# Scores on two halves of TensorE's rows, and the attention steps of a chunk dealt out to two half steps

## The chip, the cores and the metric

The kernel runs on one core of one Trainium2 chip. The time is the device time of one launch, in microseconds (us). Engines work side by side, each through its own list of instructions in order, and meet only at semaphores: TensorE (PE, with its weight loads PEld), VectorE (DVE), ScalarE (ACT), GpSimd (POOL) and SyncE (SP), which here only issues DMAs.

## The reference

The input x has 64 sequences of 128 tokens and 256 features; ctx has 192 features per token. One layer of cross attention with two softmaxes, then a quantised feed-forward layer:

```
x = x + attention(layernorm(x), ctx)      # 16 heads of 64
    q = x @ Wq + lora;  k, v = ctx[:124] @ Wk, Wv + lora
    out  = softmax(q k^T / 8) v           # the first 124 context tokens
    out += softmax(q ki^T / 8) vi         # the last 4, with Wk_ipa, Wv_ipa
    result = out @ Wo + bo + lora
x = x + ffn(layernorm(x))
    h = silu(depthwise_conv3(bitlinear(x, w1)));  bitlinear(h, w2)
```

`bitlinear` rounds its input to 8 bits by row and its weights to -1, 0, 1.

## The kernel before

**Tiling.** Four sequences make a group (`NB = 4`), so there are 16 groups. Within a group, attention goes by chunks: one sequence b and one quad q of four heads, 16 chunks to a group (`CHUNKS`). Each chunk has two half steps, so a group has 32 halves, numbered n = 0 to 31.

**Order.** Every engine has a function `steps(g, n)`, called for each group and each half, and the order of calls in it is the engine's order. Attention of group g, the projections of group g + 1 (`project`) and the feed-forward part of group g - 1 (`finish`) are interleaved by tables of half numbers (`N_Q`, `N_K`, `M_TILE`, ...). Groups 0 and 1 and the last stand unrolled; the others run in a hardware loop.

**A chunk s before**, all of it in even halves:
- PE, n = 2s: `p_v` of chunk s - 3 (L438), `transpose_p` of chunk s - 2 (L447), `scores` of chunk s (L460), `project_out` of chunk s - 4 (L473). After them and in the odd half come the projections (Q L403, K L412, V L422) and the feed-forward matmuls (L485 to L517).
- DVE, n = 2s: `attend`: the sum of the four extra exponentials and the reciprocals of chunk s - 1 (L800, L802), then the maxima of chunk s and the subtraction (L805, L806, L808). Then `project` and `finish`.
- ACT, n = 2s: the two copies of the output of chunk s - 3 (L636, L638), the copy of the transposed P of chunk s - 2 (L630), then `project` and `finish`, and at the end of the half the exponentials of chunk s (L644 four times, L647).
- POOL, n = 2s: P times the reciprocals for chunk s - 1 (L1029); in the odd half the low part of the output of chunk s - 3 (L1061).

**DVE's other work by half**, from the tables: statistics in 0 and 1; rounding of the hidden layer (L887, L894) in 1 to 3; variance in 3; `x2` (L827) in 4 and 7; normalisation in 6 to 10; V copies (L793) in 5, 14, 22 and 29; nothing in 11, 12, 13 and 31; convolution (L851, L857, L866, L871) in 15 to 27, one of these in 15 and in 27; maxima of the hidden layer (L876) in 28 and 29; scales (L880 and on) in 30. The second feed-forward matmul (L517) is in PE's halves 4 and 6; the result of 4 is used by L818 in 6, and the second run of L517 in 6 waits for that L818.

**Heads.** The keys KT of a pair of heads fill the 128 partitions, 64 for each head. A score matmul before contracts over all 128: the query tile QM holds each pair twice, with zeros in the half of the other head. ACT fills it with two copies (L611, L612), and POOL sets the zeros once at the start (L1048, L1050). P times V already writes its heads to two halves of the PSUM partitions, that is of the array's columns.

**PSUM.** Before, bank 0 holds the scores, bank 1 the transposed P, bank 2 the output of P times V, banks 3 and 4 the output product, 5 and 6 the projections, 7 the feed-forward part.

## Time and profile before

| | us |
|---|---|
| median of 3 runs (1666.96 to 1673.72) | 1671.57 |
| the profiled execution | 1673.32 |
| its span | 1671.2 |
| PE busy | 1474.9 (88%) |
| DVE busy | 1305.2 (78%) |
| ACT busy | 1183.1 (71%) |
| POOL busy | 729.1 (44%) |

The profile is of one execution. Busy time is the share of the span in which an engine has an instruction in flight; for PE the ends are modelled and neighbours overlap. "[4.32 <-PE PS L460]" behind an instruction says that its engine had been idle for 4.32 us, and that the matmul of line 460 ended the wait. DMAs move 28 GB/s on average and are of no weight in the loop.

### The profile page before, as it was taken

The page shows a single profiled execution, that of the slowest core. Times are in us where ns is not written, and L with a number is a line of the kernel's source. Part 1 is how long each engine was busy: PE and PEld are TensorE (multiplying, and loading weights), DVE is VectorE, ACT ScalarE, POOL GpSimd, SP SyncE. Part 2 cuts the span into 40 slices and gives each one's busy share as a digit, 9 for nine tenths or more (in the row PEclk, how much of TensorE's full clock was granted, in tenths as well). Part 3 has the DMA queues.
Part 4 walks back from the last instruction along what each step waited for, and adds up shares of the span by engine and source line. Part 5 has one row for each costly group of instructions (what it writes and reads, how often), then busy time and mean ns, then how long its engine had stood idle before and what let it go on. Part 6 is the DMA issues. An engine that isn't in the chain of part 4 may idle for free.

```text
span 1671.2 us, 33198 instructions
## 1 busy us (share of the span) xinstructions
PE 1474.9 (88%) x10586; PEld 1168.1 (70%) x10586; DVE 1305.2 (78%) x3157; ACT 1183.1 (71%) x3925; POOL 729.1 (44%) x1085
## 2 busy tenths in 40 slices
PE   7999999989899998989899998989999898988642
PEld 3688777777777777777777777777777777776521
DVE  4264798888878798787879888887878878787876
ACT  2477776868677786968778686867778696876521
POOL 0144445444544444444444544454444445444400
PEclk9899999999999999999999999999999999999855
DMA  7300001000000100000010100000010000000000
GB/s 187 117 28 15 28 15 42 15 25 15 26 27 13 40 13 27 13 26 27 13 40 13 40 10 27 17 26 27 13 40 13 27 13 26 27 1 26 1 13 13
DMA packets 41129, 47.14 MB, mean 28 GB/s; under 512 B 3008, under 2 KB 35200, under 8 KB 41088
## 3 DMA queue, kind: packets, MB, share of 16 engines
q1 hardware_dynamic: 40032, 45.82, 8.9%
q10 hardware_dynamic: 1056, 0.81, 0.2%
q8 instruction: 22, 0.36, 0.1%
q14 instruction: 19, 0.16, 0.0%
HBM read 36.13 MB, written 10.49 MB: 28 GB/s over the span
## 4 chain that ended last, share of the span: by engine, by line
PE 35%; DVE 32%; ACT 20%; issue 11%; DMA 0%; POOL 0%; DVEq 0%; ACTq 0%; POOLq 0%
ACT SM L644 8%; DVE GBS L876 7%; PE PS L460 6%; PE PS L422 4%; PE PS L517 4%; PE PS L403 4%; PE PS L438 4%; PE PS L447 3%; PE PS L412 3%; PE PS L473 3%; DVE GBS L887 2%; ACT H L669 2%; DVE GBS L866 2%; ACT GBS L674 2%; DVE H L894 2%
## 5 line engine op out<-in xcount | busy, mean ns | idle before, releaser
L1029 POOL TENSOR_TENSOR SM<-SM,RC 128x496 f32<-128x496 f32 (+1 forms) x512 | 340.3, 686 | 730.5 <-DVE RC L802 730.5
L644 ACT ACTIVATE SM<-PS,MX 128x124 f32<-128x124 f32 x1024 | 359.3, 365 | 200.1 <-DVE SM L808 197.1
L460 PE MATMUL PS<-KT,QM 128*128 128x128 f32 x2048 | 279.2, 279 | 26.3 <-ACT SM L644 26.2
L460 PEld LDWEIGHTS PS<-KT,QM 128*128 128x128 f32 x2048 | 249.4, 192 | 42.7 <-ACT SM L644 41.5
L1061 POOL TENSOR_TENSOR OTl<-OF,OTh 128x256 fp32r<-128x256 f32 x256 | 216.4, 846 | 5.6 <-ACT OF L638 5.6
L644 ACT ACTIVATION_READ_ACCUMULATOR SM<-PS,MX 128x1 f32 x1024 | 211.0, 206 | 0.0
L447 PE MATMUL PS<-IDF,SM 128*128 128x128 f32 x1024 | 169.3, 288 | 18.9 <-POOL SM L1029 18.8
L636 ACT ACTIVATE OTh<-PS 128x256 fp32r<-128x256 f32 x256 | 99.6, 389 | 103.2 <-PE PS L438 99.4
L438 PE MATMUL PS<-PT,V 128*64 128x128 f32 x2048 | 170.2, 288 | 0.0
L806 DVE TENSOR_REDUCE MX<-PS 128x4 f32<-128x496 f32 x256 | 169.9, 664 | 0.0
L438 PEld LDWEIGHTS PS<-PT,V 128*64 128x64 f32 x2048 | 107.8, 137 | 83.5 <-issue 77.0
L630 ACT ACTIVATE PT<-PS 128x512 f32<-128x512 f32 x256 | 155.6, 608 | 0.8 <-PE PS L447 0.7
L447 PEld LDWEIGHTS PS<-IDF,SM 128*128 128x128 f32 x1024 | 108.3, 142 | 65.5 <-issue 35.9
L473 PE MATMUL PS<-WOh,OTh 128*128 128x256 f32 x512 | 124.7, 325 | 17.1 <-POOL OTl L1061 17.1
L866 DVE TENSOR_TENSOR GBS<-PS,BC 128x512 f32<-128x512 f32 x128 | 87.5, 683 | 60.9 <-PE PS L498 58.3
L805 DVE TENSOR_REDUCE MX<-PS 128x4 f32<-128x16 f32 x256 | 41.3, 161 | 110.4 <-PE PS L460 110.4
L669 ACT ACTIVATE H<-GBS,CB,CW 128x512 f32<-128x512 f32 x128 | 105.3, 823 | 29.0 <-DVE GBS L866 27.7
L871 DVE SCALAR_TENSOR_TENSOR H<-GBS,H 128x512 f32<-128x512 f32 x128 | 103.4, 808 | 27.1 <-ACT GBS L674 27.0
L638 ACT ACTIVATE OF<-PS 128x256 f32<-128x256 f32 x256 | 99.5, 389 | 31.2 <-POOL OTl L1061 31.2
L876 DVE TENSOR_REDUCE GBS<-H 128x128 f32<-128x1024 f32 x64 | 120.5, 1928 | 0.0
L851 DVE SCALAR_TENSOR_TENSOR H<-GBS,CW,H 128x508 f32<-128x508 f32 x128 | 116.4, 909 | 0.0
L857 DVE SCALAR_TENSOR_TENSOR H<-GBS,CW,H 128x508 f32<-128x508 f32 x128 | 107.9, 843 | 10.4 <-ACT H L669 8.8
(142 smaller groups left out, 3693.8 us busy)
## 6 DMA issues: line engine op xcount, KB each, us to landing
XIN<-in_x SPq DMA_DIRECT2D x16, 512.0 KB, 3.6
XRES<-in_x SPq DMA_DIRECT2D x16, 512.0 KB, 3.5
out_y<-H SPq DMA_DIRECT2D x16, 512.0 KB, 3.0
CRAW<-in_ctxT SPq DMA_DIRECT2D x16, 256.0 KB, 2.8
RRAW<-in_ctxT SPq DMA_DIRECT2D x32, 128.0 KB, 2.8
QM<-in_Wq SPq DMA_DIRECT2D x1, 1024.0 KB, 11.0
GBS<-in_Wo SPq DMA_DIRECT2D x1, 1024.0 KB, 21.6
k_ipa_columns<-H SPq DMA_DIRECT2D x1, 1024.0 KB, 5.1
```

What stands on the lines that cost most here:

```text
L438: m = mm(psO[r:r + DH, h // 2, :], V[:, b, DH * (4 * q + h):DH * (4 * q + h) + DH], PT[:, h, :], start=True, stop=True)
L447: m = pe.transpose(psT[:, h, :], SM[c % 2][:, h, :], IDF[:])
L460: m = mm(psS[:, h, :], QM[:, 2 * q + h // 2, h % 2, TOK * b:TOK * b + TOK], KT[:, 2 * q + h // 2, b, :], start=True, stop=True)
L473: m = mm(psY[b // 2][:, b % 2, :], OT[ot][c % 2][:, a, :], WO[w][:, 2 * q + a, :], start=(q == 0 and i == 0 and b % 2 == 0), stop=(q == QU ...
L630: act.activation(PT[:], psT, ACT.Identity).then_inc(pt_done, 1)
L644: m = act.activation(SM[s % 2][:, h, 0:ORG], psS[:, h, 0:ORG], ACT.Exp, bias=MX[s % 2][:, h:h + 1], accum_out=SU[s % 2][:, h:h + 1])
L669: act.activation(H[:, j, :].rearrange("p (b t) -> p b t", b=NB), GB[j % 4], ACT.Identity, bias=CB[:, j:j + 1], scale=CW[:, j, 1:2]).then_i ...
L806: dve.tensor_reduce(MX[s % 2][:, 0:4], psS[:, :, 0:ORG], AX.X, ALU.max, negate=True)
L866: dve.tensor_tensor(GB[j % 4].rearrange("p b t -> p (b t)"), psF, BC[:], ALU.mult).then_inc(g_done, 1)
L876: dve.tensor_reduce(HM[:, b, :], H[:, :, TOK * b:TOK * b + TOK].rearrange("p j t -> p t j"), AX.X, ALU.max, apply_absolute_value=True).the ...
L1029: m = pool.tensor_tensor(part, part, RC[c % 2][:, 4 * i:4 * i + 4].unsqueeze(2).broadcast_to(shape), ALU.mult)
L1061: pool.tensor_tensor(OT[1][c % 2][:], OF[:], OT[0][c % 2][:].bitcast(F32), ALU.subtract).then_inc(ot_done, 1)
```

## The change

- **Scores.** QM becomes QT, with each pair of heads once. A head's scores contract over its own 64 partitions, on its own half of the array's rows; even heads write PSUM bank 0, odd heads bank 1. ACT needs one copy of a query tile in place of two (128 partitions in place of twice 64), and the zeros go. A tile STAGE takes over the weight staging that QM did at the start.
- **Banks.** The scores hold banks 0 and 1, so the transposed P moves to bank 2, the bank that the output of P times V lies in. So `transpose_p` now waits for the output copies of the chunk before (`ot_high`), and `p_v` no longer does.
- **Halves.** `transpose_p` and `scores` (PE), the copy of the transposed P and the exponentials (ACT) and the maxima and the subtraction (DVE, now the function `maxima`) move to the odd half n = 2s + 1. `p_v`, `project_out`, the output copies, the sums and reciprocals (DVE, now `sums`) and POOL's steps stay in the even one.

```diff
-        psS = PS[:, 0, :].rearrange("p (h k) -> p h k", h=4)
-        psT = PS[:, 1, :].rearrange("p (h k) -> p h k", h=4)
+        psS = PS[:, 0:2, 0:2 * TOK].rearrange("p r (a k) -> p r a k", a=2)
+        psT = PS[:, 2, :].rearrange("p (h k) -> p h k", h=4)
...
# PE, p_v
-                    need(pe, ot_high, gc.count(CHUNKS, c))
...
# PE, transpose_p
                     pe.wait_ge(p_done, gc.count(CHUNKS, c + 1))
+                    need(pe, ot_high, gc.count(CHUNKS, c))
...
# PE, scores
-                        m = mm(psS[:, h, :], QM[:, 2 * q + h // 2, h % 2, TOK * b:TOK * b + TOK],
-                               KT[:, 2 * q + h // 2, b, :], start=True, stop=True)
+                        rows = slice(DH * (h % 2), DH * (h % 2) + DH)
+                        m = mm(psS[:, h % 2, h // 2, :], QT[rows, 2 * q + h // 2, TOK * b:TOK * b + TOK],
+                               KT[rows, 2 * q + h // 2, b, :], start=True, stop=True)
...
# PE, steps
                 if n % 2 == 0:
                     p_v(g, n // 2)
+                    project_out(g, n // 2)
+                else:
                     transpose_p(g, n // 2)
                     scores(g, n // 2)
-                    project_out(g, n // 2)
...
# ACT, project
-                        act.activation(QM[0:64, 2 * q + a, 0, :], psU[u % 2][0:64, :], ACT.Identity)
-                        act.activation(QM[64:128, 2 * q + a, 1, :], psU[u % 2][64:128, :], ACT.Identity).then_inc(unit_free[u % 2], 1)
+                        act.activation(QT[:, 2 * q + a, :], psU[u % 2], ACT.Identity).then_inc(unit_free[u % 2], 1)
...
# ACT, steps
                 if n % 2 == 0:
                     output_copies(g, n // 2)
+                else:
                     transposed_copy(g, n // 2)
...
-                if n % 2 == 0:
+                if n % 2 == 1:
                     exponentials(g, n // 2)
...
# DVE, steps
                 if n % 2 == 0:
-                    attend(g, n // 2)
+                    sums(g, n // 2)
+                else:
+                    maxima(g, n // 2)
...
# POOL, at the start
-            pool.memset(QM[0:64, :, 1, :], 0.0).then_inc(zeroed, 1)
-            pool.wait_ge(zeroed, 1)
-            pool.memset(QM[64:128, :, 0, :], 0.0).then_inc(zeroed, 1)
```

The DVE's list in halves 4 and 5 of a group, before: SU and RC are the sums and reciprocals, MX and the SM row the maxima and the subtraction.

```order
L800 TENSOR_REDUCE SU<-SM 128x4 [waits exp_done]
L802 RECIPROCAL RC<-SU 128x8 [waits sum_done]
L804 REGISTER_ALU
L805 TENSOR_REDUCE MX<-PS 128x4 [waits s_full]
L806 TENSOR_REDUCE MX<-PS 128x4
L808 TENSOR_TENSOR SM<-PS,MX 128x4x4 [waits max_done]
L823 REGISTER_ALU
L824 ISA [waits y_done]
L120 REGISTER_ALU [waits xres_done]
L827 TENSOR_TENSOR X<-PS,XRES 128x512 [waits copy_done]
L792 ISA
L793 COPY V<-PS 124x2x256 [waits unit_full]
```

The same place on the DVE in the changed kernel (lines are some 1 to 3 higher there).

```order
L801 TENSOR_REDUCE SU<-SM 128x4 [waits exp_done]
L803 RECIPROCAL RC<-SU 128x8 [waits sum_done]
L826 REGISTER_ALU
L827 ISA [waits y_done]
L120 REGISTER_ALU [waits xres_done]
L830 TENSOR_TENSOR X<-PS,XRES 128x512 [waits copy_done]
L807 REGISTER_ALU
L808 TENSOR_REDUCE MX<-PS 128x4 [waits s_full]
L809 TENSOR_REDUCE MX<-PS 128x4
L811 TENSOR_TENSOR SM<-PS,MX 128x4x4 [waits max_done]
L793 ISA
L794 COPY V<-PS 124x2x256 [waits unit_full]
```

The maxima moved from right behind the sums to behind the even half's other work, so that only the odd half's work (here the copy of V) stands between them and the next sums.

ACT's list from half 12 to 14, before: OTh and OF are the two output copies, PT the transposed P, the SM rows the exponentials, Q1T a copy of the feed-forward part.

```order
L636 ACTIVATE OTh<-PS 128x256 [waits o_full]
L638 ACTIVATE OF<-PS 128x256 [waits ot_done]
L630 ACTIVATE PT<-PS 128x512 [waits t_full]
L616 REGISTER_ALU
L617 ACTIVATE KT<-PS 128x4x124 [waits unit_full]
L642 REGISTER_ALU
L644 ACTIVATE SM,SU<-PS,MX 128x124 [waits sub_done]
L644 ACTIVATE SM,SU<-PS,MX 128x124 x3
L647 ACTIVATE SM<-SM 128x4x4
L636 ACTIVATE OTh<-PS 128x256 [waits o_full]
L638 ACTIVATE OF<-PS 128x256 [waits ot_done]
L630 ACTIVATE PT<-PS 128x512 [waits t_full]
```

ACT in the changed kernel, from half 12 to 14.

```order
L636 ACTIVATE OTh<-PS 128x256 [waits o_full]
L638 ACTIVATE OF<-PS 128x256 [waits ot_done]
L616 REGISTER_ALU
L617 ACTIVATE KT<-PS 128x4x124 [waits unit_full]
L630 ACTIVATE PT<-PS 128x512 [waits t_full]
L642 REGISTER_ALU
L644 ACTIVATE SM,SU<-PS,MX 128x124 [waits sub_done]
L644 ACTIVATE SM,SU<-PS,MX 128x124 x3
L647 ACTIVATE SM<-SM 128x4x4
L636 ACTIVATE OTh<-PS 128x256 [waits o_full]
L638 ACTIVATE OF<-PS 128x256 [waits ot_done]
```

The copy of PT and the exponentials now stand at the two ends of an odd half, and the output copies follow the exponentials directly.

PE's list from the second feed-forward product in half 4 on, before.

```order
L517 MATMUL PS<-W,H 128x256 [waits q2_done]
L517 MATMUL PS<-W,H 128x256 x15
L403 MATMUL PS<-XTh,WQh 128x512 [waits unit_free1]
```

PE at the same place in the changed kernel.

```order
L518 MATMUL PS<-W,H 128x256 [waits q2_done]
L518 MATMUL PS<-W,H 128x256 x15
L447 MATMUL PS<-IDF,SM 128x128 [waits ot_high,p_done]
L447 MATMUL PS<-IDF,SM 128x128 x3
L120 REGISTER_ALU
L461 MATMUL PS<-KT,QT 128x128 [waits s_used]
L461 MATMUL PS<-KT,QT 128x128 x3
L403 MATMUL PS<-XTh,WQh 128x512 [waits unit_free1]
```

The transposes and scores moved from ahead of that product (they stood at the start of half 4, and stand next at the start of half 6) to right behind it.

## Rows read from the trace of the kernel before

**Rows 1.** Busy us by engine in one stretch, instructions; clock, DMA share, GB/s.

```profile
800.00:900.00 100.00, 92.25 (x691) 74.25 (x690) 83.74 (x206) 77.23 (x260) 47.76 (x71) 1.00 0.07 22
```

**Rows 2.** Timeline, DVE: start, us, line, operation; L805 of group 2, then of 15.

```profile
248.89 0.17 DVE L805 TENSOR_REDUCE MX<-PS 128x4 f32<-128x16 f32 x1 [1.43 <-PE PS L460]
...
1492.15 0.17 DVE L805 TENSOR_REDUCE MX<-PS 128x4 f32<-128x16 f32 x1
```

**Rows 3.** Waits between 700 and 1000 us: who for whom, total us, times, longest.

```profile
ACT SM L644 <- DVE SM L808: 36.9, 21, 4.6
...
DVE MX L805 <- PE PS L460: 15.3, 19, 1.9
...
DVE SU L800 <- ACT SM L647: 6.4, 6, 1.7
```

**Rows 4.** Timeline, DVE, first two chunks of group 0.

```profile
85.88 0.17 DVE L805 TENSOR_REDUCE MX<-PS 128x4 f32<-128x16 f32 x1 [4.32 <-PE PS L460]
...
88.39 0.17 DVE L800 TENSOR_REDUCE SU<-SM 128x4 f32<-128x16 f32 x1 [0.35 <-ACT SM L647]
...
89.50 0.17 DVE L805 TENSOR_REDUCE MX<-PS 128x4 f32<-128x16 f32 x1 [0.70 <-PE PS L460]
```

**Rows 5.** Timeline, ACT, first chunk of group 0.

```profile
86.75 0.37 ACT L644 ACTIVATE SM<-PS,MX 128x124 f32<-128x124 f32 x1 [0.77 <-DVE SM L808]
...
88.13 0.23 ACT L647 ACTIVATE SM<-SM 128x16 f32<-128x16 f32 x1
```

**Rows 6.** Timeline, ACT, a chunk of the loop.

```profile
863.87 0.23 ACT L647 ACTIVATE SM<-SM 128x16 f32<-128x16 f32 x1
863.98 0.39 ACT L636 ACTIVATE OTh<-PS 128x256 fp32r<-128x256 f32 x1
864.24 0.40 ACT L638 ACTIVATE OF<-PS 128x256 f32<-128x256 f32 x1
```

**Rows 7.** Timeline, PE, a chunk of the loop.

```profile
839.76 0.40 PE L403 MATMUL PS<-XTl,WQh 128*128 128x512 f32 x1
839.99 0.40 PE L403 MATMUL PS<-XTh,WQl 128*128 128x512 f32 x1
840.32 0.66 PE L438 MATMUL PS<-PT,V 128*64 128x128 f32 x8
840.91 0.66 PE L447 MATMUL PS<-IDF,SM 128*128 128x128 f32 x4
841.40 1.06 PE L460 MATMUL PS<-KT,QM 128*128 128x128 f32 x8
842.21 0.48 PE L473 MATMUL PS<-WOh,OTh 128*128 128x256 f32 x2
```

**Rows 8.** Timeline, DVE, the same chunk.

```profile
842.50 0.17 DVE L805 TENSOR_REDUCE MX<-PS 128x4 f32<-128x16 f32 x1 [1.86 <-PE PS L460]
```

**Rows 9.** Timeline, PE, the second feed-forward product.

```profile
837.07 1.92 PE L517 MATMUL PS<-W,H 128*128 128x256 bf16 x16 [0.45 <-DVE H L894]
838.75 0.47 PE L403 MATMUL PS<-XTh,WQh 128*128 128x512 f32 x1
```

**Rows 10.** Timeline, PE, half 13.

```profile
860.76 0.28 PE L422 MATMUL PS<-WVh,CTh 128*128 128x256 f32 x1
...
861.93 0.62 PE L485 MATMUL PS<-IDB,H 128*128 128x128 bf16 x8
```

**Rows 11.** Timeline, DVE, half 28.

```profile
811.34 3.85 DVE L876 TENSOR_REDUCE GBS<-H 128x128 f32<-128x1024 f32 x2
```

**Rows 12.** Timeline, DVE and POOL, the convolution.

```profile
880.02 1.23 DVE L871 SCALAR_TENSOR_TENSOR H<-GBS,H 128x512 f32<-128x512 f32 x1
...
882.90 0.68 DVE L871 SCALAR_TENSOR_TENSOR H<-GBS,H 128x512 f32<-128x512 f32 x1
...
879.48 1.22 POOL L1061 TENSOR_TENSOR OTl<-OF,OTh 128x256 fp32r<-128x256 f32 x1
```

**Rows 13.** Lines of ACT: count, busy us, mean ns, idle before.

```profile
L612 ACT ACTIVATE QM<-PS 64x512 f32<-64x512 f32 x128 | 75.9, 593 | 1.5
```

More of the change, by code:

```diff
@@ L170, in program @@
         CTR = sb("CTR", [P, T], F32R)
-        QM = sb("QM", [P, PAIRS, 2, T])
+        QT = sb("QT", [P, PAIRS, T])
+        STAGE = sb("STAGE", [P, 4096])
         KT = sb("KT", [P, PAIRS, NB, TOK])
@@ L224, in program @@
         kv_full, kv_used, ipa_out = sem("kv_full"), sem("kv_used"), sem("ipa_out")
-        zeroed = sem("zeroed")
         x_in, c_in = sem("x_in"), sem("c_in")
@@ L260, in program @@
         kipa_dram = nc.dram_tensor("k_ipa_columns", [GROUPS, P, PAIRS * NB * IPA], F32, kind="Internal").ap()
-        qm_flat = QM[:].rearrange("p a b t -> p (a b t)")
-        wq_raw = qm_flat[:, 0:2048].rearrange("p (k n) -> p k n", k=2)
-        wk_raw, wkr_raw, wv_raw, wvr_raw = (qm_flat[:, 2048 + 1024 * i:3072 + 1024 * i] for i in range(4))
-        q_up_t, k_up_t = (qm_flat[:, 6144 + 1024 * i:7168 + 1024 * i] for i in range(2))
+        wq_raw = STAGE[:, 0:2048].rearrange("p (k n) -> p k n", k=2)
+        q_up_t, k_up_t = (STAGE[:, 2048 + 1024 * i:3072 + 1024 * i] for i in range(2))
+        qt_flat = QT[:].rearrange("p a t -> p (a t)")
+        wk_raw, wkr_raw, wv_raw, wvr_raw = (qt_flat[:, 1024 * i:1024 * i + 1024] for i in range(4))
         kt_flat = KT[:].rearrange("p a b t -> p (a b t)")
@@ L438, in p_v @@
                         m = mm(psO[r:r + DH, h // 2, :], V[:, b, DH * (4 * q + h):DH * (4 * q + h) + DH],
-                               PT[:, h, :], start=True, stop=True)
+                               PT[:, 2 * (h % 2) + h // 2, :], start=True, stop=True)
                     m.then_inc(o_full, 1)
@@ L563, in _ @@
                 project(At(0), n)
-            pe.wait_ge(zeroed, 2)
             pe.wait_ge(w_low, len(splits))
@@ L643, in exponentials @@
                     for h in range(4):
-                        m = act.activation(SM[s % 2][:, h, 0:ORG], psS[:, h, 0:ORG], ACT.Exp, bias=MX[s % 2][:, h:h + 1],
+                        m = act.activation(SM[s % 2][:, h, 0:ORG], psS[:, h // 2, h % 2, 0:ORG], ACT.Exp, bias=MX[s % 2][:, h:h + 1],
                                            accum_out=SU[s % 2][:, h:h + 1])
@@ L794, in project, with sums @@
                                     psU[u % 2][0:ORG, :].rearrange("p (b n) -> p b n", b=2)).then_inc(unit_free[u % 2], 1)
-            def attend(g, s):
+            def sums(g, s):
                 gc, c = chunk_at(g, s - 1)
@@ L802, in attend, with maxima @@
                     dve.reciprocal(RC[c % 2][:], SU[c % 2][:]).then_inc(rec_done, 1)
+            def maxima(g, s):
                 if g.exists():
                     dve.wait_ge(s_full, g.count(CHUNKS, s + 1))
-                    dve.tensor_reduce(MX[s % 2][:, 4:8], psS[:, :, ORG:TOK], AX.X, ALU.max, negate=True).then_inc(max_done, 1)
-                    dve.tensor_reduce(MX[s % 2][:, 0:4], psS[:, :, 0:ORG], AX.X, ALU.max, negate=True)
+                    dve.tensor_reduce(MX[s % 2][:, 4:8].rearrange("p (r a) -> p r a", r=2), psS[:, :, :, ORG:TOK], AX.X, ALU.max, negate=True).then_inc(max_done, 1)
+                    dve.tensor_reduce(MX[s % 2][:, 0:4].rearrange("p (r a) -> p r a", r=2), psS[:, :, :, 0:ORG], AX.X, ALU.max, negate=True)
                     dve.wait_ge(max_done, g.count(CHUNKS, s + 1))
-                    dve.tensor_tensor(SM[s % 2][:, :, ORG:TOK], psS[:, :, ORG:TOK],
-                                      MX[s % 2][:, 4:8].unsqueeze(2).broadcast_to([P, 4, IPA]), ALU.add).then_inc(sub_done, 1)
+                    dve.tensor_tensor(SM[s % 2][:, :, ORG:TOK].rearrange("p (r a) k -> p r a k", r=2), psS[:, :, :, ORG:TOK],
+                                      MX[s % 2][:, 4:8].rearrange("p (r a) -> p r a", r=2).unsqueeze(3).broadcast_to([P, 2, 2, IPA]), ALU.add).then_inc(sub_done, 1)
             def finish(g, n):
@@ L1044, in _ @@
                 project(At(0), n)
-            pool.wait_ge(w_low, 6)
-            pool.wait_ge(du_used, DU_O)
-            pool.memset(QM[0:64, :, 1, :], 0.0).then_inc(zeroed, 1)
-            pool.wait_ge(zeroed, 1)
-            pool.memset(QM[64:128, :, 0, :], 0.0).then_inc(zeroed, 1)
-            pool.wait_ge(zeroed, 2)
             pool.wait_ge(du_used, DU_N)
```

## The prediction

> **What bounds the kernel now.** First the busy time of the engines in a stretch of the loop [rows 1]: TensorE (PE) 92.3 us of 100, VectorE (DVE) 83.7, ScalarE (ACT) 77.2, at the full granted clock (1.00). None is full. PE's busy time counts overlapping matmuls double, so the DVE, whose operations run one behind the other, is the better ruler. The time of one group of 16 chunks comes from the first and last start of the small maximum (L805) over groups 2 to 14, which run all stages together [rows 2]: (1492.15 - 248.89) / 13 = 95.6 us, 5.98 us per chunk. Of these the DVE works 95.6 x 0.84 = 80.3 us and idles 15.3 us. The waits of 300 us [rows 3] show that it idles little for anything: 15.3 us for the scores in 19 waits, 6.4 us for the exponentials in 6, while ACT waits for the DVE's subtraction 36.9 us in 21. So the DVE leads; ACT and PE follow, and each has slack to it because the DVE's sums read exponentials which ACT made a whole half (two halves are one chunk) earlier.
>
> I therefore write the time of a group as DVE work plus DVE idle; the work stays, and the idle time is built anew for the changed order.
>
> **The serial chain.** In group 0 nothing else delays the chunks, and their pieces can be read off [rows 4, 5]. From L805 (85.88) to the first exponential (86.75) is 0.87 us; the last one's end lets the DVE start its sums at 88.39, so L805 to L800 takes 2.5 us. The next L805 comes at 89.50: 3.6 us per chunk is the shortest cycle before.
>
> After the change two things lengthen it. First, the exponentials of a chunk are the last thing in ACT's odd half, and the sums are the first thing in the DVE's next even half: in the odd half the DVE can hide only 2.5 - 0.73 (its maxima, L805 to the next operation) = 1.77 us by its own work. Second, the transposes now share bank 2 with P times V, and wait for `ot_high`. ACT makes the two output copies right after the exponentials. In the loop [rows 6], after L647 starts (863.87), L636 and L638 follow at 0.11 and 0.37 us, L638 lasts 0.40, so the copies are done 0.77 us after L647's start. Sums begin 0.26 us after L647's start [rows 4, 5], so the copies end 0.5 us behind the sums' start. Then transposes to scores 0.49 us (840.91 to 841.40), scores to L805 1.10 us (841.40 to 842.50) [rows 7, 8]. Scores on two halves of the rows change only the last number. Behind the waiting transposes stand the scores, and the DVE's maxima wait for these.
>
> **Price of the scores.** Eight matmul passes of four heads take 0.81 us (841.40 to 842.21), 0.10 us each. No row shows two row halves. The nearest is P times V, on two halves of the columns: eight passes in 0.59 us (840.32 to 840.91), 0.07 us each, though with half as many weight columns. If the halves overlap fully, 0.40 us go: scores to L805 0.7 us. If they don't overlap and PE has to switch its layout in and out, it costs what entering P times V costs more than a plain step, (840.32 - 839.99) - (839.99 - 839.76) = 0.10 us, and as much again: 1.3 us. I take 1.0 us, nearer to the P times V row. So from the sums' start to the next L805 are 0.5 + 0.05 + 0.49 + 1.0 = 2.0 us (1.7 to 2.3); less the sums (0.3), the DVE can hide 1.7 us by its even half. The shortest chunk becomes 2.5 + 2.0 = 4.5 us.
>
> The Trainium skill, TensorEngine Tiling, Key Properties, says that a change of tiling mode drains TensorE; the rows of P times V agree with a small cost, 0.10 us. By full overlap, as its Theoretical Speedup has it (up to twice), the chunk would be 4.2 us, by drains alone 4.8.
>
> **Idle of the DVE per group, half by half** (n is the half; the work in each follows from the placement numbers). The terms are what of 1.8 us (exponentials, odd half) and of 1.7 us (next scores, even half) the work there leaves open.
>
> - 31 and 0: no work in 31, 0.7 us in 0 (two statistics): 1.8 + 1.0 = 2.8.
> - 3 and 4: the second output product (L517) waits for the DVE's rounding, takes 1.7 us (837.07 to 838.75) [rows 9], and now stands ahead of the transposes of half 5: 1.7 + 0.5 + 1.0 + 0.1 = 3.3 us behind the rounding, in which the DVE has 1.4 us of work: 1.9.
> - 5 and 6: 0.6 us of work in 5 leaves 1.2; in 6 the next L517 waits for L818 behind the sums, and the transposes again for it: 0.8 + 3.3 us against 2.1 of work: 2.0. Together 3.2.
> - 11 and 12: no work at all: 1.8 + 1.7 = 3.5.
> - 13 and 14: PE sets the pace. Projection of V 1.17 (860.76 to 861.93), transposes 0.6 (L485) [rows 10], then Q 1.4 (six steps of 0.23), the broadcast 0.9 (an estimate: two passes of a float32 matmul four times as long as a score pass), P times V and product 1.4, less 0.3 because they start ahead of L805 (842.21 against 842.50), transposes and scores 1.5: 6.7 us against 1.0 + 0.6 of the DVE: 5.0.
> - 15 and 16: in the same way 5.9 us of PE against 3.7: 2.2.
> - 25 and 26: 1.4 us of work in each, 0.4 + 0.3 = 0.7. 27: one operation of 0.6, 1.2. 30: L880 needs PE's transposes of the maxima, which the DVE's own maxima of scores hid before: 0.5.
> - 1, 2, 7 to 10, 17 to 24, 28, 29: the work is longer than what is to be hidden (two L876 alone are over 3.7 us [rows 11]): 0.
>
> Sum 21.0 us. Added to it is 1.2 us of slower DVE work: L871 took 0.68 us alone and 1.23 us beside L1061 on GpSimd [rows 12]. The multiplication L1029 ran beside the maxima, which read PSUM; now it runs beside the even half's work from SBUF. Bounds 0 and 0.5 x 16 = 8 us; I take 0.3 us in each of the four conv chunks.
>
> A group: 80.3 + 21.0 + 1.2 = 102.5 us, 6.9 more than 95.6 (22.2 us of idle and slowed time in place of 15.3). Times 13: 90. Groups 1 and 15 have most stages: 5 each. Group 0 is bound by PE and this chain, 3 us. Sum 103 us.
>
> **What costs nothing.** ACT saves one copy of 0.59 us per tile (L612, 128 of them, 75.9 us) [rows 13]; ACT waits for the DVE anyway, so it only waits more. The memsets of the query tile (GpSimd, 3.5 us each) lie beside the first projections. DMAs are unchanged in size and time.
>
> The profiled execution took 1673.3 us, 2.1 us beyond its span, and 1.7 over the median shown. 1673.3 + 103 = 1776 us.
>
> **The rivals.**
> - Faster: the scores leave the path. The DVE's waits for L460 [rows 3] are 15.3 us in 3 groups, 5.1 per group, and if ACT and DVE hide the handshake by the slack of the next half, those go: 16 x 5 = 80 us at most, of which I would keep 40: 1635. For it: PE is the busiest. Against: the exponentials and sums adjoin, and no slack is left there. It decides if the DVE finds the exponentials finished in halves 12 and 0. 0.11.
> - No change: the PE saving pays for the handshake, 1665 to 1681. 0.05.
> - Halves don't run together: 0.3 us more in the seven chunks where the scores are on the path, and 0.1 in others: 3 us a group, about 1825. For it: the switch rows; against: the cheaper passes of P times V. 0.17.
> - GpSimd contention in every chunk: 5 us a group more, 1850. The slowed L871 speaks for it, the many DVE operations that read PSUM against. 0.05.
> - Mild: full overlap (0.3 less in seven chunks) and PE running ahead in 3 to 6: 3 us a group less, 1725. 0.22.
>
> The forecast itself, 1750 to 1800, has 0.40. Range: 1670 to 1830, which leaves out the faster case, the contended one and little else. This kernel's measurement tells about 0.5% (8 us) from no change. Faster 0.11, same 0.05, slower 0.84.
>
> **What would show it.** L801 (sums) waiting for ACT's exponentials in over half of the chunks, some 1.2 to 1.8 us each in halves 0, 6, 12, 28; the transposes waiting for ACT's L638; the shortest chunk 4.5 us; eight score passes in 0.4 to 0.8 us; DVE busy down to 78 of 100. I am wrong if sums still rarely wait, or if the group takes under 97 us.

## The result, and the profile after

The changed kernel takes 1844.6 us (median of 4 runs, 1842.4 to 1846.4) against 1671.4 us for the kernel before (4 runs): a ratio of 1.104, 95% interval [1.102, 1.106]. The direction was forecast, the size not: 173 us in place of 103, beyond the upper end of 1830. The profiled execution's span is 1842.6 us, and the mean granted clock 0.929 (before 0.967).

The view of busy time by engine over the same 100 us as in [rows 1], of the changed kernel (columns as there):

```profile
800.00:900.00 100.00, 85.07 (x614) 64.31 (x610) 76.83 (x180) 63.20 (x218) 44.48 (x65) 0.95 0.07 22
```

Every engine is less busy: PE 92 to 85, DVE 84 to 77, ACT 77 to 63. No engine became the bound; all of them wait more. Of the last three figures (granted clock, DMA share, GB/s) the first has fallen too: 0.95 where it was 1.00.

The period of a group, from the small maximum (now L808) of groups 2 and 15, as in [rows 2]:

```profile
261.91 0.17 DVE L808 TENSOR_REDUCE MX<-PS 128x4 f32<-128x16 f32 x1 [1.17 <-PE PS L461]
...
1654.18 0.17 DVE L808 TENSOR_REDUCE MX<-PS 128x4 f32<-128x16 f32 x1 [1.82 <-PE PS L461]
```

The first row starts at 261.91 and the other at 1654.18: (1654.18 - 261.91) / 13 = 107.1 us, forecast 102.5, before 95.6. Who waits for whom between 700 and 1000 us, as in [rows 3]:

```profile
ACT SM L644 <- DVE SM L811: 50.4, 39, 4.9
...
DVE MX L808 <- PE PS L461: 32.2, 14, 5.1
...
DVE SU L801 <- ACT SM L647: 20.8, 17, 1.7
PE PS L447 <- ACT OF L638: 19.8, 13, 4.8
DVE H L860 <- ACT H L669: 10.8, 12, 1.4
```

ACT waits for the DVE's subtraction in nearly every chunk, and the DVE for ACT's exponentials in 17 of some 45: 20.8 us where [rows 3] had 6.4. The prediction had asked for over half of the chunks. Over the whole run it is 106 chunks of 256, 127.5 us, 1.2 us each: the length came out as forecast, the number of chunks did not. The third row from the top of this list is the handshake that was forecast, the next the shared bank. The last is one that was not.

The DVE's intervals from one L808 to the next, named by their odd half (31 is the one with half 0 in it), forecast and then the mean over groups 2 to 14, in us:

| 31 | 1 | 3 | 5 | 7 | 9 | 11 | 13 |
|---|---|---|---|---|---|---|---|
| 4.5 | 8.7 | 5.9 | 7.1 | 6.2 | 8.7 | 4.5 | 6.7 |
| 4.72 | 9.07 | 5.80 | 7.09 | 6.18 | 9.58 | 5.42 | 7.96 |

| 15 | 17 | 19 | 21 | 23 | 25 | 27 | 29 |
|---|---|---|---|---|---|---|---|
| 5.9 | 5.8 | 6.2 | 6.8 | 5.5 | 4.6 | 6.6 | 8.4 |
| 6.01 | 5.64 | 6.70 | 6.42 | 6.62 | 4.85 | 6.52 | 8.50 |

The prediction doesn't list these intervals. The forecast line was worked out after the result, from the prediction's idle terms and the DVE's work in each interval; this work adds up to 81.1 us, where the prediction has 80.3. Nine of the sixteen lie within 0.25 us of it. Four are over 0.8 us off: 9, 11, 13 and 23. They make 4.2 of the 5.0 us between the sums of the two lines (102.1 and 107.1; the prediction's own sum, with its contention, was 102.5).

Halves 12 to 14 on PE, from its timeline (start, us, line, tiles; in brackets the idle time before), in one group (interval 13 takes 8.54 us here, more than its mean):

```profile
835.26 0.39 PE L474 MATMUL PS<-WOh,OTl 128*128 128x256 f32 x2
838.97 1.09 PE L447 MATMUL PS<-IDF,SM 128*128 128x128 f32 x4 [3.31 <-ACT OF L638]
839.98 1.23 PE L461 MATMUL PS<-KT,QT 64*128 64x128 f32 x8
841.14 0.58 PE L422 MATMUL PS<-WVh,CTh 128*128 128x256 f32 x1
...
843.44 1.08 PE L486 MATMUL PS<-IDB,H 128*128 128x128 bf16 x8
...
848.51 0.60 PE L447 MATMUL PS<-IDF,SM 128*128 128x128 f32 x4
849.04 0.71 PE L461 MATMUL PS<-KT,QT 64*128 64x128 f32 x8
849.69 0.50 PE L412 MATMUL PS<-CTh,WKh 128*128 128x512 f32 x1
```

and the busy times by stretch there (PE, PEld, DVE, ACT, POOL, then the granted clock):

```profile
836.00:838.00 2.00, 0.00 (x0) 0.00 (x0) 0.64 (x2) 1.32 (x8) 0.00 (x0) 1.00 0.83 218
838.00:840.00 2.00, 1.03 (x6) 0.73 (x6) 0.37 (x2) 1.30 (x6) 1.20 (x3) 0.63 0.13 44
840.00:842.00 2.00, 2.00 (x13) 1.78 (x13) 0.74 (x3) 0.60 (x1) 1.09 (x4) 0.50 0.00 0
842.00:844.00 2.00, 2.00 (x14) 1.91 (x14) 0.30 (x4) 1.60 (x9) 0.00 (x0) 0.50 0.00 0
844.00:846.00 2.00, 2.00 (x17) 1.53 (x16) 0.75 (x2) 0.43 (x2) 1.19 (x2) 0.67 0.00 0
846.00:848.00 2.00, 2.00 (x11) 1.58 (x10) 0.00 (x0) 1.14 (x2) 1.43 (x2) 1.00 0.00 0
```

PE idles 3.31 us, since the transposes wait for ACT's copy of O. In this group the granted clock is 0.50, the 1.2 GHz level, for about 6.8 us: all of 840 to 844 and, by the clocks 0.63 and 0.67, some 1.5 and 1.3 us of the windows on both sides, so that it fell before the idle time was over. The same transposes and scores, T and S below, take 1.01 and 1.16 us there (838.97 to 839.98 to 841.14), and 0.53 and 0.65 at full clock (848.51 to 849.04 to 849.69). The stretch lies in the intervals 11 (835.81 to 841.26) and 13 (to 849.80), in which little of the DVE's work hides it.

Interval by interval, in groups 2 to 14, three things show that this is more than one bad group. The clock is under 1 in intervals 11 and 13 of every group (0.50 to 0.81 and 0.75 to 0.91 on average), and 13 takes 7.31 us where the clock is back early and up to 8.63 where it is late. It also falls in other places: in half 9 of seven groups, here at about 828 us behind gaps of only 0.76 and 1.05 us, which costs nothing, since interval 9 takes 9.58 us with and without it; and in interval 29 and 31 of nine groups, of which interval 31 takes 4.72 us or more, against 4.47 in the four groups at full clock. In the kernel before the clock was 1.00 through all of groups 2 to 14 but for a few us at the end of the first of them.

### The profile page after: what moved, and what is told of

It is laid out like the page before. It is cut to its first block, busy times and chain, and to the rows that moved or that the text cites. A ratio compares the mean times of both kernels' runs of the same rounds, so it can differ in the third digit from the quotient of the medians.

```text
span 1842.6 us, 33129 instructions
## 1 busy us (share of the span) xinstructions
PE 1520.8 (83%) x10586; PEld 1131.4 (61%) x10586; DVE 1337.1 (73%) x3157; ACT 1106.6 (60%) x3797; POOL 743.9 (40%) x1083
## 4 chain that ended last, share of the span: by engine, by line
DVE 36%; PE 33%; ACT 18%; issue 12%; DMA 0%; DVEq 0%; POOL 0%; ACTq 0%; POOLq 0%
ACT SM L644 9%; DVE GBS L879 6%; PE PS L422 5%; PE PS L461 4%; PE PS L403 3%; PE PS L447 3%; PE PS L518 3%; DVE H L874 3%; PE PS L474 3%; PE PS L412 3%; DVE GBS L890 3%; ACT H L669 3%; DVE MX L809 3%; DVE H L897 2%; PE PS L437 2%
## 5 line engine op out<-in xcount | busy, mean ns | idle before, releaser
L1034 POOL TENSOR_TENSOR SM<-SM,RC 128x496 f32<-128x496 f32 (+1 forms) x512 | 364.0, 732 | 872.7 <-DVE RC L803 872.7
L447 PEld LDWEIGHTS PS<-IDF,SM 128*128 128x128 f32 x1024 | 125.8, 149 | 164.4 <-issue 156.2
L1060 POOL TENSOR_TENSOR OTl<-OF,OTh 128x256 fp32r<-128x256 f32 x256 | 212.3, 829 | 7.5 <-ACT OF L638 7.0
L461 PE MATMUL PS<-KT,QT 64*128 64x128 f32 x2048 | 197.1, 314 | 0.7 <-ACT SM L644 0.7
L808 DVE TENSOR_REDUCE MX<-PS 128x4 f32<-128x16 f32 x256 | 43.2, 169 | 196.4 <-PE PS L461 195.9
L474 PE MATMUL PS<-WOh,OTh 128*128 128x256 f32 x512 | 130.7, 337 | 65.5 <-POOL OTl L1060 65.3
L461 PEld LDWEIGHTS PS<-KT,QT 64*128 64x128 f32 x2048 | 145.2, 200 | 48.1 <-issue 46.5
L860 DVE SCALAR_TENSOR_TENSOR H<-GBS,CW,H 128x508 f32<-128x508 f32 x128 | 117.6, 919 | 54.6 <-ACT H L669 54.4
L474 PEld LDWEIGHTS PS<-WOh,OTh 128*128 128x128 f32 x512 | 77.7, 191 | 115.5 <-POOL OTl L1060 82.1
L801 DVE TENSOR_REDUCE SU<-SM 128x4 f32<-128x16 f32 x256 | 41.8, 163 | 127.5 <-ACT SM L647 127.5
L669 ACT ACTIVATE H<-GBS,CB,CW 128x512 f32<-128x512 f32 x128 | 106.4, 831 | 27.2 <-DVE GBS L869 27.2
L403 PE MATMUL PS<-XTh,WQh 128*128 128x512 f32 x256 | 111.3, 435 | 1.2 <-DVE XTl L789 1.2
```

What stands on the lines that cost most here:

```text
L403: m = mm(bank, WQ[w][:, k, P * tile:P * tile + P], XT[xt][:, k, :], start=(i == 0), stop=(i == 5))
L447: m = pe.transpose(psT[:, h, :], SM[c % 2][:, h, :], IDF[:])
L461: m = mm(psS[:, h % 2, h // 2, :], QT[rows, 2 * q + h // 2, TOK * b:TOK * b + TOK], KT[rows, 2 * q + h // 2, b, :], start=True, stop=True)
L474: m = mm(psY[b // 2][:, b % 2, :], OT[ot][c % 2][:, a, :], WO[w][:, 2 * q + a, :], start=(q == 0 and i == 0 and b % 2 == 0), stop=(q == QU ...
L669: act.activation(H[:, j, :].rearrange("p (b t) -> p b t", b=NB), GB[j % 4], ACT.Identity, bias=CB[:, j:j + 1], scale=CW[:, j, 1:2]).then_i ...
L1034: m = pool.tensor_tensor(part, part, RC[c % 2][:, 4 * i:4 * i + 4].unsqueeze(2).broadcast_to(shape), ALU.mult)
```

## The experiments

Theories: A, the handshake of exponentials and sums (the prediction's); C, the granted clock behind PE's idle time; others as the texts say (a text may give its letters another sense). Each kernel was timed beside the kernel before (medians 1668.9 to 1672.1 us), and each ratio is to that. The edits are shown in outline.

**1. The new dealing alone, and with the shared bank.** Padded Q and a bank each for T and O, only the steps dealt to halves as in the change:

```
-  even: p_v, transpose_p, scores, project_out; attend (sums + maxima)
+  even: p_v, project_out; sums     odd: transpose_p, scores; maxima
```

> The kernel before with the new dealing out of the steps to even and odd halves alone: padded queries, scores over all rows, and three separate banks for scores, transposes and output. Theory A (exponentials and sums now adjoin, the transposes wait for the output copies, and TensorE's idle time behind that wait lowers its granted clock): only the first part is here, so some 5 us a group of the 11.5, 1740 to 1770 us, granted clock in the loop 1.00. Rival B (the row halves of the scores are what costs): 1840 us with these halves alone is excluded, the time stays within 1% of before, 1665 to 1690. Rival C (the handshake alone is all of it): 1830 to 1850.

Measured 1850.7 us, ratio 1.109 [1.107, 1.110]: the dealing alone costs 181 us, the whole loss and more. Both A (1740 to 1770, clock 1.00) and B are refuted; the time is at the edge of C's range, but the clock fell here too, so the handshake isn't all of it. The second kernel adds `psT = PS[:, 2, :]` and moves the wait for `ot_high` to the transposes:

> As the kernel of the halves alone, and the transposed P in the bank of the output of P times V, with the wait of the transposes for the output copies. Theory A: with this wait the gap of TensorE in half 12 and the half clock behind it are there: 1835 to 1870 us, loop clock 0.95. Rival B (row halves): as the kernel without the shared bank, within 1%.

Measured 1881.6 us, 1.127 [1.125, 1.129]: 31 us for the bank, above A's range as well. From there to the changed kernel, row halves and unpadded Q take 37 us off. So +181 + 31 - 37 = +175, against 173 measured (the kernel before was 1.7 us faster beside these two).

**2. PE kept busy in half 12**, behind the output product, by matmuls whose result nobody reads; 22 of them, then 44:

```
+  if n == 12: for i in range(22): mm(psF[:, 0:256], WQ[0][:, 0, 0:P], XT[0][:, 0, 0:256])
```

> The changed kernel with 22 extra matmuls of 256 columns, whose result nobody uses, behind the output product in half 12 of each group, where TensorE otherwise idles 3.3 us. Theory A (clock): the granted clock stays at 1.00 through halves 12 to 14, the two chunks around take 4.5 and 6.7 us in place of 5.4 and 8.5, 2.5 to 3 us less in 14 groups: 1800 to 1815 us. Rival D (the clock falls but TensorE is off the path there): 1840 to 1850, or more by the extra work.

Measured 1827.3 us, 1.094 [1.092, 1.096]: 17 us less, outside the ranges of both theories (1800 to 1815, 1840 to 1850). In nine groups of 13 some 2.16 us of idle time were left, and the clock still fell, for about 3.4 us in the group of the last two rows below. In the other four it had fallen in half 9, PE came late to the extra matmuls, only some 0.7 us of idle time were left (0.69 in this group), and the clock stayed at 1.00. Interval 11, then 13, in one group of these four and in one of the nine (columns as above):

```profile
723.92:728.39 4.47, 3.78 (x34) 3.31 (x34) 1.20 (x6) 3.22 (x13) 1.49 (x5) 1.00 0.34 119
728.39:735.05 6.66, 6.66 (x53) 5.25 (x54) 1.80 (x6) 3.78 (x14) 3.38 (x6) 1.00 0.00 0
828.51:833.25 4.74, 2.58 (x22) 2.02 (x20) 1.20 (x6) 3.22 (x13) 1.76 (x6) 0.92 0.20 71
833.25:841.18 7.93, 7.93 (x53) 6.48 (x54) 1.80 (x6) 3.83 (x14) 3.15 (x5) 0.83 0.00 0
```

All four groups at full clock agree to 0.01 us: 4.47 and 6.66, where the changed kernel has means of 5.42 and 7.96.

> The changed kernel with 44 more matmuls of 256 columns behind the output product of half 12 (22 took 17 us off and left 2.16 us of idle TensorE, behind which the granted clock still fell). Theory C (the 3.3 us in which TensorE idles in half 12 let the granted clock fall, and halves 13 to 15 then run at half speed): the 44 take 5.4 us at full clock, the idle time is filled, no window of halves 12 to 15 shows a clock under 1.00, halves 13-14 take 6.7-7.5 us; halves 11-12 grow by at most 1 us since the matmuls end later than the wait did; time 1790-1830. Rival (the gap was not the cause of the clock): clock under .7 remains near half 14 and the time is 1840-1870.

Measured 1827.6 us, 1.094 [1.091, 1.096]. PE's timeline and the windows of that stretch:

```profile
826.70 5.37 PE L581 MATMUL PS<-XTh,WQh 128*128 128x256 f32 x44
831.91 0.60 PE L447 MATMUL PS<-IDF,SM 128*128 128x128 f32 x4
832.43 0.71 PE L461 MATMUL PS<-KT,QT 64*128 64x128 f32 x8
```

```profile
830.00:832.00 2.00, 2.00 (x19) 2.00 (x18) 0.37 (x2) 1.95 (x10) 0.56 (x1) 1.00 0.00 0
832.00:834.00 2.00, 2.00 (x20) 1.72 (x19) 0.80 (x3) 0.60 (x1) 1.75 (x6) 1.00 0.00 0
834.00:836.00 2.00, 2.00 (x25) 1.68 (x24) 0.30 (x3) 1.93 (x11) 0.00 (x0) 1.00 0.00 0
```

More work, and less time: in all 13 groups the clock stays at 1.00 in halves 12 to 14, T takes 0.52 us, and interval 13 falls from 7.96 to 6.67 us, the forecast's 6.7. This is C's range. The clock's share is shown: 1.3 us in interval 13, 0.95 in 11 (5.42 less 4.47) and 0.25 in 31 (4.72 less 4.47), 2.5 us per group, 33 us in 13 groups. No run got back more than 17 of them. Here the transposes of interval 11 stand behind the matmuls (4.73 us in ten groups, 6.1 to 6.2 in the three in which the clock fell in half 9), and falls in other halves lengthen intervals 3 and 29 by 0.3 and 0.1 us.

**3. ScalarE's order.** In half 23 the DVE stands at L860 for ACT's H copy (L669):

```profile
878.78 1.29 DVE L860 SCALAR_TENSOR_TENSOR H<-GBS,CW,H 128x508 f32<-128x508 f32 x1 [1.22 <-ACT H L669]
```

The edit puts `finish` ahead of `project` on ACT.

> The changed kernel with one edit on ScalarE: in every half the steps of the feed-forward stage come ahead of the projection's copies. Theory A (in half 23 VectorE waits 1.2 us at line 860 for ScalarE's H copy, which stands behind exponentials, O or PT copies and the K copy, so that 23 takes 6.6 us in place of 5.5, and 19 takes 6.7 in place of 6.2): 23 falls to 5.5-6.0 and 19 to 6.2-6.5, VectorE's waits of 54 us for ScalarE's H copies to under 30, and other halves grow by less than 0.5 us; time from 1845 to 1815-1840. Rival (ScalarE's order is only shifted: TensorE then waits for the K, Q and V copies, which free the banks of its projections): new waits of TensorE for ScalarE at those banks of 30 us or more, time 1840-1870.

Measured 1827.1 us, 1.093 [1.090, 1.096]; interval 23 from 6.62 to 5.88 us, 19 unchanged at 6.71; waits for H copies 54.4 to 34.5 us. Of the 1.34 us per group 0.75 are interval 23's. Another 0.52 are interval 13's (7.96 to 7.44), at a mean clock of 0.86 to 0.90, so this edit too moved the clock's fall. The same edit on the kernel before:

> The kernel before with ScalarE's feed-forward steps ahead of its projection copies. In the kernel before VectorE waits 8.8 us at line 857 for the H copies and 27 us each at lines 871 and 887 for ScalarE's tanh and scale copies, 63 us in all. Theory A (ScalarE's order is a debt of the new dealing alone): 1660-1680, no difference. Rival (VectorE's waits for ScalarE are on the path here too): 1635-1660. Third (TensorE then waits for the banks that the projection copies free): 1680-1720.

Measured 1670.9 us (10 runs), 1.0004 [0.999, 1.002]: there ACT's order was free, as A said. Not because nothing moved: intervals 27 and 15 fell by 0.6 and 0.3 us and 31 grew by 0.8.

**4. Experiments 2 (with 44) and 3 together.**

> The changed kernel with both edits that took 17 us off alone: 44 extra matmuls behind the output product of half 12, and ScalarE's feed-forward steps ahead of its projection copies. If the two shares are separate (halves 13-14 from 7.96 to 6.67, half 23 from 6.62 to 5.88): both intervals show their new values at once, 104.0-104.8 us per group and 1805-1815 us. If one stall feeds both: 1820-1830. If the order of ScalarE makes the matmuls' stage late: 1830 or more.

Measured 1827.3 us, 1.093 [1.091, 1.095]. Both intervals show their new values (13: 6.67, 23: 5.87), but 11 takes 6.10 us in place of 5.42, as the transposes stand behind the matmuls. In twelve of 13 groups the clock fell in half 9 (in three of 13 with the matmuls alone), the matmuls start late, and interval 11 takes 6.2 us; in the thirteenth it takes 4.73. The two causes are apart; the remedies get in each other's way. The time is that of the text's second case, one stall for both, and would have misled; the intervals don't.

**5. GpSimd beside the DVE.** Its multiplication cut to 32 and 8 columns; this kernel leaves most attention weights undivided:

> The changed kernel with GpSimd's multiplication cut from 496 and 16 columns to 32 and 8, so the attention weights stay undivided in most columns (its output is not the reference's); every step and wait stays. Theory A (VectorE's operations at lines 760 and 763 in half 9 take 0.93 and 0.75 us because this multiplication runs beside them): they take under 0.3 us and halves 9-10 take 8.5-8.8 in place of 9.58; over all halves 1 to 2 us per group less, time 1810-1835. Rival (the length of these two is their own in this place, or the low part of O is what runs beside them): 9-10 stay above 9.3 and the time within 10 us of 1845.

Measured 1815.1 us, 1.087 [1.084, 1.089]. The DVE's small operation of half 9, first in the changed kernel, then here:

```profile
831.42 0.93 DVE L760 TENSOR_SCALAR AD<-AM,WD 128x4 f32<-128x4 f32 x1
```

```profile
819.70 0.23 DVE L760 TENSOR_SCALAR AD<-AM,WD 128x4 f32<-128x4 f32 x1
```

The interval 9 falls from 9.58 to 8.80, the forecast's 8.7; L760 shows the contention plainly. L763 hardly moves (0.75 to 0.67), and L785 takes 1.21 us where it took 0.69: beside both now runs GpSimd's low part of O (L1060). Over the group 1.9 us are gone, within the range of theory A; interval 1 fell as much as 9 (9.07 to 8.29), others moved both ways. The multiplication moved instead of cut, to the odd half behind the low part of O:

> The changed kernel with only GpSimd's multiplication by the reciprocals moved to the odd half (behind the low part of O); the sums stay in the even half. Theory A (VectorE's operations at lines 760 and 763 in half 9 take 0.93 and 0.75 us in place of 0.23 and 0.17 because GpSimd's multiplication runs beside them, and halves 9-10 take 9.6 us in place of 8.7): they fall to below 0.35 us and 9-10 to 8.7-8.9; other pairs of halves move by under 0.3 us; time 1820-1845. Rival (the multiplication is only put beside other operations of VectorE, 1.23 in place of 0.68 us for the copies of H as in half 13): the sum over halves stays within 0.5 us, time 1840-1860.

Measured 1878.5 us, 1.125 [1.121, 1.128]: interval 9 falls to 9.05, but 1, 3 and 7 grow by 0.8, 1.5 and 1.1, and the time is above both ranges. L785 takes 1.41 us in place of 0.69 beside it, as the rival said. That is not all: GpSimd now stands 683 us for ACT's copies of O with the multiplication behind it. How much is contention and how much this wait was not separated.

**6. The handshake taken away, in six kernels.** Sums and multiplication in the odd half ahead of the maxima:

> The changed kernel with the sums and reciprocals of a chunk, and GpSimd's multiplication, in the next odd half instead of the even one, so that the sums again have a half of slack to the exponentials; bank sharing stays. Theory A: VectorE's waits for the exponentials (127 us) go, those for the scores stay; of 11.5 us a group about 5 to 6 come back: 1740 to 1770 us. Rival E (the shared bank alone sets the cycle, as exponentials, output copies, transposes and scores are one chain anyway): 1820 to 1850.

Measured 1921.8 us, 1.148 [1.143, 1.154]. Theory A failed here by a new wait: PE stood 272 us for GpSimd's low part of O, which stood behind the moved multiplication. With the low part ahead of the multiplication, on the changed kernel and on the dealing alone:

> The changed kernel with the sums (and GpSimd's multiplication) moved to the odd half, ahead of the maxima, a half later than the exponentials that they read, and with GpSimd's low part of O ahead of its multiplication, so that the 272 us in which TensorE waited for that low part in the run called sums_late can go. Theory A (the cost of the new dealing is that the exponentials end an odd half and the sums begin the very next half, so VectorE stands 127 us for them): VectorE's waits for the exponentials fall from 127 us below 40, and the time falls from 1845 to 1740-1790. Rival B (the cost is that the scores are read only in an odd half while everything that feeds them sits there too, so VectorE's wait moves to the scores): waits for the exponentials fall, VectorE's wait for the scores rises from 196 us to 280 or more, and the time stays at 1830-1880. Rival C (the granted clock): halves 11 to 15 keep their 5.45 + 8.54 us and 1820-1850 comes out.

> The same placing of the sums, of the multiplication and of the low part, but on the kernel before with only the new dealing of halves (padded Q, a bank each for T and O). Theory A: from 1851 us to 1730-1790, since there TensorE has no wait for O's copies ahead of the transposes. Rival B: 1830-1880. If this one falls and sums_late2 does not, the shared bank is what holds the changed kernel back once the sums are late.

Measured 1826.8 us, 1.094 [1.092, 1.096], and 1806.7 us, 1.082 [1.080, 1.084]: 18 and 44 us less, where A had 1740 to 1790 and 1730 to 1790; the first also kept intervals 11 and 13 at 4.98 and 7.66 us, at a clock of 0.85 to 0.89. Then the sums left in the even half, but as its last step:

> The changed kernel with the sums and reciprocals moved within the even half from VectorE's first step to its last; nothing else. Theory A (the exponentials end ScalarE's odd half and the sums open VectorE's next half, so VectorE stands 1.2 us in 106 halves, 127 us in all; of these some are only moved to the next wait): the waits for the exponentials go to under 10 us, and the time falls by 40 to 110 us, to 1735-1805. Rival B (VectorE's idle time is set by the ring exponentials, scores, maxima and by TensorE's arrival at the scores, so what VectorE gains in the even half it loses at the maxima of the odd one): waits for the exponentials go, waits for the scores rise by as much, 1825-1850. Rival D (GpSimd's multiplication, now later, ends too late for its low part of O and TensorE's output product): TensorE's waits for the low part rise from 65 us to over 120, 1850 or more.

Measured 1908.2 us, 1.143 [1.140, 1.146]: the low part again, the text's case D (a row of the waits: who, total, times, longest).

```profile
PE PS L474 <- POOL OTl L1060: 267.8, 150, 4.1
```

> sums_end with the 44 extra matmuls behind the output product of half 12 and with ScalarE's feed-forward steps ahead of its projection copies, which took 17 us each alone. If they add up: 34 us below sums_end. If the clock's fall and ScalarE's lateness are fed by the same stall of VectorE for the exponentials: 0 to 20 us below sums_end. Theory A as a whole (these three are what the new dealing costs beyond its scores' gain): 1700-1770. Rival (a cost is still unnamed): 1775-1815.

Measured 1982.9 us, 1.188 [1.182, 1.193], a miss: the extra matmuls stand behind an output product that is itself late, and interval 11 takes 9.39 us. Last, the low part in the even half ahead of the multiplication:

> sums_end with GpSimd's low part of O in the even half ahead of the multiplication, so that it no longer stands behind the late reciprocals. Theory A (VectorE's standing of 127 us for the exponentials is a cost of the new dealing of its own): TensorE's waits for the low part fall from 268 us to under 60, VectorE's for the exponentials stay under 65, the time falls to 1760-1815, below the changed kernel's 1845. Rival B (what VectorE gains there it loses at the scores, whose ring of exponentials, scores and maxima it does not shorten): waits for the scores over 280 us, 1825-1860. Rival D (GpSimd still ends too late, now for the transposes): TensorE waits over 60 us for the multiplication, 1860 or more.

Measured 1826.2 us, 1.092 [1.090, 1.095]. Waits here:

```profile
DVE MX L808 <- PE PS L461: 247.2, 92, 5.1
...
PE PS L447 <- ACT OF L638: 118.7, 88, 6.3
...
DVE SU L801 <- ACT SM L647: 56.0, 46, 1.7
```

The DVE's waits for the exponentials fell by 71 us (127.5 to 56.0), those for the scores rose by 51 (195.9 to 247.2). The time fell by 18. This is rival B in time (1825 to 1860) and in kind, though the wait for the scores stayed under its 280 us: most of what is freed at one end of the ring is waited for at the other.

**7. P times V, the copies of O and its low part moved to the odd half**, a half ahead of where P times V was, with the changed kernel's rows and bank, and then on the kernel before:

```
-  even: p_v, transpose_p, scores, project_out
+  even: transpose_p, scores, project_out     odd: p_v (and the copies and low part of O)
```

> The changed kernel's row halves, unpadded Q and shared bank with the roles of the halves exchanged: transposes, scores, output product, exponentials, sums and maxima all in even halves as before the change, and P times V with the copies and the low part of O in odd halves. Theory A (adjacency of exponentials and sums is the cost): the exponentials again end an even half and the sums begin the next even one, VectorE's waits for them fall from 127 us to 20 or less as in the kernel before, and the cheaper scores (0.65 in place of 0.81 us for 8 passes) and unpadded Q remain: 1640-1690. Rival B (any order in which P times V is a half away from the transposes costs, because PT and OT are handed over later and the bank is shared): 1700-1800. Rival C: halves 12 to 14 show a granted clock under .7 and 1690-1720 comes out.

> The kernel before with one edit: P times V, the copies of O and the low part move to the odd half (one half ahead of where they were); padded Q, a bank each for T and O, everything else in the even halves. It stands beside pv_odd (1759 us), which has the row halves, unpadded Q and the shared bank on top. Theory A (in pv_odd the shared bank is what costs: TensorE waits 133 us for O's copies ahead of the transposes, which stand on ScalarE behind the exponentials of the half before): without it 1660-1690, the wait gone. Rival (P times V in the odd half costs by itself, as PT and O cross a half's end between TensorE and ScalarE once more): 1720-1770.

Measured 1758.9 us, 1.053 [1.051, 1.055], and 1765.3 us, 1.055 [1.049, 1.060]. Theory A's numbers failed in both, and the rivals' ranges (1700 to 1800, 1720 to 1770) hold: this move costs 94 us by itself, and the bank, the row halves and the unpadded Q together take 6 off, so that the bank's own price in this order isn't shown. The waits of the second:

```profile
POOL OTl L1063 <- ACT OF L639: 492.6, 239, 5.3
...
PE PS L447 <- POOL SM L1031: 51.0, 34, 3.2
```

GpSimd stands in the odd half for ACT's copy of O, which before was made in the half ahead; the multiplication of the next half stands behind it, and PE's transposes wait for that. But the interval that grew most is 31, from 3.86 to 6.61 us, 36 of the 94 us, and in it the clock is 0.55 on average in all 13 groups (before 1.00 in twelve of them). In one group:

```profile
858.00:860.00 2.00, 1.51 (x8) 1.18 (x10) 1.81 (x7) 0.48 (x3) 1.17 (x2) 0.50 0.00 0
860.00:862.00 2.00, 2.00 (x14) 1.67 (x11) 1.86 (x10) 2.00 (x10) 0.27 (x2) 0.50 0.00 0
862.00:864.00 2.00, 2.00 (x12) 2.00 (x11) 0.28 (x2) 0.16 (x2) 1.73 (x3) 0.50 0.00 0
```

PE works through these windows at the 1.2 GHz level, and the maxima start only at 865.28. So a moved step can cost by where the clock then falls, and not only by the wait that it adds.

**8. Unpadded Q and row halves in the old dealing**, all heads in one bank, with a wait of PE between heads 0, 2 and 1, 3:

```
+  if h == 1: m.then_inc(s_even, 1); pe.wait_ge(s_even, ...)
```

> The kernel before, in its own order of halves, with Q unpadded and the scores on two halves of array rows, but all four heads in one bank as before: heads 0 and 2 first, then TensorE waits for them by a semaphore of its own, then heads 1 and 3, so the row halves never run side by side and T and O keep their banks. It leaves ScalarE one copy of Q (512 columns) in place of two, 128 of them fewer over the run, 76 us of its 1183 busy. Theory A (the loss of the change is all in the dealing of halves and in the shared bank; ScalarE's saved copies are a gain of their own): 1640-1668. Rival (TensorE's wait within the scores takes 0.3-0.6 us per chunk, 256 times, on the path of VectorE's maxima, and ScalarE was not the bound): 1675-1750. Within 0.5%: 1663-1680 if both are small.

Measured 1777.2 us, 1.064 [1.061, 1.066]; the rival's mechanism, above its range. PE's timeline:

```profile
847.32 1.48 PE L465 MATMUL PS<-KT,QT 64*128 64x128 f32 x8
848.72 0.50 PE L478 MATMUL PS<-WOh,OTh 128*128 128x256 f32 x2
```

The scores take 1.40 us in place of 0.81 [rows 7], 0.59 more, 151 us over 256 chunks, and 106 show in the time, with unpadded Q's saving in them: 0.70 us per us. By that rate the 0.16 us saved in the changed kernel (0.81 to 0.65) would be worth 29 us, an estimate, of the 37 measured in experiment 1.

None of the eighteen kernels is faster than the kernel before, and the one on a par with it is the kernel before with ScalarE's steps exchanged.

## Why the prediction was too low

- **The view of the kernel was right.** The DVE leads, and a group is its work plus its idle time. The DVE's idle and slowed time was forecast at 22.2 us per group; 107.1 less 80.3 is 26.8. One reason given for it was wrong, though: PE's busy time doesn't count overlapping matmuls double, since a window of 2 us reads at most 2.00 (840 to 842 above) while the matmuls in it overlap.
- **The shortest chunk was right, by two errors that cancel.** Forecast 4.5 us, measured 4.47 in interval 31 of the four groups at full clock. From the sums' start to the next L808 it had 2.0 us. Transposes and scores to L808 take 0.53 + 0.76 at full clock (848.51 to 849.04 above, and L808 starts at 849.80) where 0.49 + 1.0 stood, and behind the end of L638 PE starts 0.15 us later, not 0.05.
- **The price of the scores (1.0 us to L808) was too high.** 0.65 us for eight passes, where full overlap had 0.4 and none 0.8. The first step behind them takes 0.33 us where 0.23 is plain, but behind the full-row scores it took 0.32 too (842.21 to 842.53), so no price of the switch shows. The rival in which the halves don't run together is refuted.
- **The step that failed: "13 and 14: PE sets the pace", 6.7 us.** Its terms took PE's passes at full clock, and so did the chain behind "11 and 12: no work at all: 1.8 + 1.7 = 3.5", in which PE too has nothing to do but wait. I did not ask what this wait does to the granted clock. Measured are 7.96 us for interval 13 and 5.42 for 11; at full clock they are 6.66 and 4.47 (experiment 2), as forecast. With 0.25 us in interval 31 the clock is 2.5 us of the 5.0 between the two sums, a term that the prediction didn't have.
- **"23 and others: the work is longer than what is to be hidden: 0"** failed in 23 by 1.1 us, of which ACT's order is 0.75 (experiment 3). I counted the DVE's work against two waits only, and not against ACT's own lateness: "ACT waits for the DVE anyway" holds on average, and not in the chunks of the convolution.
- **Contention (1.2 us, put into the convolution)** was in the wrong place. It is 0.8 us in half 9 (experiment 5), where operations of 0.2 us take 0.9; the convolution's four operations have means of 919, 818, 681 and 826 ns, 3.24 us together, as before (843, 909, 683 and 808 ns), and 3.09 with the multiplication cut. So what contention they have was there before the change.
- **The sum of these:** clock 2.5, half 9 0.8, ACT's order 0.75, together 4.05 of the 5.0 us; the rest wasn't traced.
- **The groups at the ends** were forecast at 13 us; the measured total, 171 us of span, less 13 x 11.5 leaves 22, 9 of the 70 us by which the total was too low. No experiment looked at them.
- **The handshake is real, but not a price of its own.** The prediction's sign rests on it, and so do the six of the nine intervals above for which it had idle terms (31, 3, 5, 15, 25, 27); the other three are the DVE's work alone. Yet where experiment 6 took it away by better than half, 18 us (44 without the shared bank) came back, and the DVE's wait moved to the scores. That the dealing costs 181 us is shown; that it does so because each chunk now crosses from DVE to ACT and back within one half is argued. Some 33 us of the changed kernel's loss (13 x 2.5, an estimate) are the clock's. Which of the crossings in PE's, ACT's and GpSimd's orders takes how much of the rest stays open; experiment 7 shows that a move of P times V and what hangs on it costs 94, at least in part through the clock.

## What to carry to other kernels

In a pipeline of in-order engines, price a moved step by the slack between each producer and consumer before and after, interval by interval, and for every engine in the ring, GpSimd too; a wait that is taken away mostly returns at the next crossing. Where a forecast leaves TensorE without work as here (2.2 to 4.8 us in half 12), work out the next microseconds, and the last of the wait, a second time at the half clock; and look at every interval of every group, since a mean hides a fall that comes in some groups only. And a view by intervals tells which terms were wrong when the total can't.

## What the runs showed of the hardware

- Around 3.31 us of idle PE (4.76 in the group before it) the granted clock was 0.50 for about 6.8 us; with 2.16 us (22 matmuls) it fell too, for about 3.4. With the dealing alone it fell around 3.57 us. It also fell for about 3.4 us behind gaps of 0.76 and 1.05 us, in seven groups of 13; in the others the same steps ran at 1.00.
- Scores on two row halves, each in a bank of its own: 0.65 us for eight passes, 0.81 on the full rows; with a semaphore wait between the halves, 1.40.
- DVE operations on 128x4 elements beside GpSimd's multiplication: 0.93 us where 0.23 is usual. One of 64x512 that takes 0.69 took 1.41 beside the multiplication and 1.21 beside the low part of O. The longer one doubled, the short one quadrupled.
